# A fused Perceiver block on one Trainium2 core: the third batch's value leaf sum on TensorE, and its attention's last steps moved

## What is computed

```
x = x + xattn(layernorm(x), ctx, ctx)                     # 16 heads of 64, context 4 x 2048 x 128
x = x + retention(layernorm(x))                           # 8 heads of 16: Q K^T * decay, V, group norm, silu gate, W_O
x = x + ffn(layernorm(x))
...
def _fff(x, nw, nb, w1, b1, w2, b2, act):                 # 8 decisions choose one of 256 leaves for each row
    for _ in range(DEPTH):
        node = 2 * node + 1 + (logit > 0)
    h = act(einsum('bsd,bsdl->bsl', x, w1[leaf]) + b1[leaf])        # 16 hidden values for each row
    return einsum('bsl,bsld->bsd', h, w2[leaf]) + b2[leaf]          # the leaf sum: 16 weighed blocks and a bias
...
q, k, v = _fff(xn, ...q), _fff(xn, ...k), _fff(xn, ...v)
att = softmax(q @ k.T / sqrt(D))
y = xn + att @ v
return y + _fff(y, ...f, gelu)
```

## Time and profile before

| what | us |
|---|---|
| median of 3 runs | 679.15 (678.81 to 680.03) |
| the profiled execution, its own time | 679.74 |
| its span in the profile | 677.5 |
| PE busy | 608.1 (90%) |
| DVE busy | 450.5 (66%) |
| ACT busy | 394.6 (58%) |
| POOL busy | 280.4 (41%) |

### The profile page before, as it was taken

How to read it: one execution, slowest core, us unless ns; L and a number is a source line. 1 busy time by engine, 2 the same in 40 slices (tenths; PEclk the granted TensorE clock), 3 DMA queues, 4 the chain that set the end, 5 groups by cost and what they waited for, 6 DMA issues and landing times.

```text
span 677.5 us, 10771 instructions
## 1 busy us (share of the span) xinstructions
PE 608.1 (90%) x4122; PEld 536.2 (79%) x4122; DVE 450.5 (66%) x799; ACT 394.6 (58%) x837; POOL 280.4 (41%) x267
## 2 busy tenths in 40 slices
PE   5899999999999999898999999989999998865664
PEld 3688888999998989777988898777989897744554
DVE  1666656777776776776777777776778776842833
ACT  2765555677664555866556855957557755521541
POOL 3210002021110207996162438876161548944832
PEclk9999999999999999998999999999999999975795
DMA  9710000020100008130030045300300052103812
GB/s 200 218 33 1 1 0 1 1 63 32 32 1 1 1 2 320 31 99 1 1 129 1 1 147 239 118 13 1 126 4 1 5 222 99 66 1 128 352 51 119
DMA packets 21401, 48.52 MB, mean 72 GB/s; under 512 B 1508, under 2 KB 14696, under 8 KB 17256
## 3 DMA queue, kind: packets, MB, share of 16 engines
q0 software_dynamic: 4608, 34.74, 13.6%
q1 hardware_dynamic: 16024, 12.79, 7.1%
q10 hardware_dynamic: 720, 0.33, 0.2%
HBM read 47.59 MB, written 0.26 MB: 71 GB/s over the span
## 4 chain that ended last, share of the span: by engine, by line
PE 65%; POOL 16%; DVE 7%; ACT 6%; issue 3%; DMA 2%; ACTq 0%; POOLq 0%; DVEq 0%
PE ps_s L428 24%; PE ps_av L428 20%; PE ps_ring L648 13%; POOL leaf L1417 6%; PE ps_m L428 4%; PE ps_ring L428 3%; POOL leaf L1421 3%; ACT prob L977 2%; POOL leaf L1458 2%; DVE chunk_max L1268 2%; POOL ct_lo L1386 1%; DVE pt_lo L1062 1%; ACT pt_hi L905 1%; DMA leaf<-up_f_dram,idx 1%; POOL leaf L1399 1%
## 5 line engine op out<-in xcount | busy, mean ns | idle before, releaser
L905 ACT CAST pt_hi<-ps_ring 128x512 fp32r<-128x512 f32 x256 | 144.5, 590 | 149.5 <-PE ps_ring L648 147.3
L1062 DVE TENSOR_TENSOR pt_lo<-ps_ring,pt_hi 128x512 fp32r<-128x512 f32 x256 | 170.4, 686 | 63.2 <-ACT pt_hi L905 63.1
L648 PE MATMUL ps_ring<-ident,prob 128*128 128x128 f32 x1024 | 145.2, 274 | 14.5 <-DVE x_sb L1300 4.9
L977 ACT ACTIVATE prob<-ps_s,neg_max 128x1024 f32<-128x1024 f32 x128 | 141.7, 1113 | 27.4 <-DVE neg_max L1351 27.2
L1268 DVE TENSOR_REDUCE chunk_max<-ps_s 128x1 f32<-128x1024 f32 x128 | 150.7, 1216 | 4.5 <-PE ps_s L428 4.4
L428 PE MATMUL ps_av<-pt_hi,c_hi 128*128 128x256 f32 x512 | 151.3, 295 | 0.0
L648 PEld LDWEIGHTS ps_ring<-ident,prob 128*128 128x128 f32 x1024 | 117.2, 141 | 41.3 <-issue 23.6
L428 PE MATMUL ps_av<-pt_lo,c_hi 128*128 128x256 f32 x512 | 144.7, 283 | 0.0
L428 PE MATMUL ps_av<-pt_hi,c_lo 128*128 128x256 f32 x512 | 144.6, 282 | 0.0
L428 PE MATMUL ps_s<-ct_hi,q_hi 128*128 128x512 f32 x256 | 113.4, 443 | 5.1 <-ACT prob L977 3.5
L428 PE MATMUL ps_s<-ct_hi,q_lo 128*128 128x512 f32 x256 | 102.1, 399 | 0.0
(11 more groups left out here) (264 smaller groups left out, 747.5 us busy)
## 6 DMA issues: line engine op xcount, KB each, us to landing
stage<-ctx_t_dram SPq DMA_DIRECT2D x16, 256.0 KB, 3.4
stage<-ctx_rows_dram SPq DMA_DIRECT2D x16, 256.0 KB, 3.0
leaf<-w_v_dram SPq DMA_DIRECT2D x1, 512.0 KB, 8.1
leaf<-w_o_dram SPq DMA_DIRECT2D x1, 512.0 KB, 10.8
dec<-decay_dram SPq DMA_DIRECT2D x1, 512.0 KB
nw<-node_w_dram SPq DMA_DIRECT2D x1, 510.0 KB
wsm<-w_small_dram SPq DMA_DIRECT2D x1, 448.0 KB
leaf<-wq_t_dram SPq DMA_DIRECT2D x1, 384.0 KB, 11.3
```

What stands on the lines that cost most here:

```text
L648: last = nc.tensor.transpose(o[:, i * P:(i + 1) * P], prob[:, n % 2, k:k + P], ident[:])
L905: nc.scalar.copy(pt_hi[:, pp, row:row + KPC, P * (n % 2):P * (n % 2 + 1)], ps_ring[:, i % 2, :].rearrange("p (k q) -> p k q", k=KPC)).then ...
L977: nc.scalar.activation(prob[:, n % 2, 1024 * e:1024 * (e + 1)], ps_s[:, 1024 * e:1024 * (e + 1)], ACT.Exp, bias=neg_max[:, n:n + 1], accum ...
L1062: return nc.vector.tensor_tensor(o, a, b_, op)
```

## The change

The third batch's value leaf sum goes from POOL to PE. `value_sum(True)` (step `v_half`) adds the bias and the 8 blocks that POOL has weighed, `value_sum(False)` (step `v_rest`) the 8 blocks that ACT has weighed, in a free part of the PSUM bank `ps_av`; ACT then copies the sum to `tree[:, 2, :]` (`v_sum_copy`). POOL's `fold2` and `out2` of this batch get the number 1000, which no slot has: they are not issued. The numbers of steps of the third batch behind the scores of its attention are raised: `attv`, `y`, `res`, `y_t`, `logits_f`, `turns_f`, `path_f`, `pick_f`.

```diff
 BEFORE_LAST_AT = {
-    ("PE", "qk_t"): 72, ("PE", "att"): 73, ("PE", "attp_t"): 76, ("PE", "attv"): 76, ("PE", "y_t"): 78,
-    ("PE", "logits_f"): 79, ("PE", "path_f"): 80,
-    ("ACT", "qk_t"): 73, ("ACT", "att"): 76, ("ACT", "attp_t"): 77, ("ACT", "y_t"): 78, ("ACT", "gelu"): 91,
+    ("PE", "qk_t"): 72, ("PE", "att"): 73.5, ("PE", "v_half"): 73, ("PE", "v_rest"): 76, ("PE", "attp_t"): 76, ("PE", "attv"): 77.5, ("PE", "y_t"): 80,
+    ("PE", "logits_f"): 81, ("PE", "path_f"): 82,
+    ("ACT", "qk_t"): 73, ("ACT", "att"): 76, ("ACT", "attp_t"): 77, ("ACT", "v_sum_copy"): 78, ("ACT", "y_t"): 81, ("ACT", "gelu"): 91,
...
-    ("DVE", "attmax"): 75, ("DVE", "y"): 77, ("DVE", "turns_f"): 80, ("DVE", "pick_f"): 82, ("DVE", "hid3"): 90,
-    ("Pool", "res"): 78, ("Pool", "gather3"): 83, ...
+    ("DVE", "attmax"): 75, ("DVE", "y"): 80, ("DVE", "turns_f"): 82, ("DVE", "pick_f"): 83, ("DVE", "hid3"): 90,
+    ("Pool", "res"): 82, ("Pool", "gather3"): 83, ...
...
-    ("Pool", "fold2"): 74,
-    ("Pool", "out2"): 74,
+    ("Pool", "fold2"): 1000,
+    ("Pool", "out2"): 1000,
 }
...
+            def value_sum(by_pool):
+
+                rows, o = down_rows_at(B - 2, 2), ps_av[:, 2 * P:3 * P]
+                if by_pool:
+                    pe.wait_ge(S["av_taken"], PAIRS)
+                    pe.wait_ge(S["got_down2"], 16 * (B - 1))
+                    mm(o, ident[:], rows[:, W1:DOWN_ROW], True, False)
+                    pe.wait_ge(S["v_weighed"], 1)
+                    for l in range(LW // 2, LW):
+                        mm(o, ident[:], rows[:, D * l:D * (l + 1)], False, False)
+                else:
+                    pe.wait_ge(S["weighed"], 4 * (B - 2) + 3)
+                    for l in range(LW // 2):
+                        last = mm(o, ident[:], rows[:, D * l:D * (l + 1)], False, l == LW // 2 - 1)
+                    last.then_inc(S["v_summed"], 1)
...
+                elif k in ("v_half", "v_rest"):
+                    value_sum(k == "v_half")
...
+                elif k == "v_sum_copy":
+                    act.wait_ge(S["v_summed"], 1)
+                    nc.scalar.copy(tree[:, 2, :], ps_av[:, 2 * P:3 * P]).then_inc(S["v_out_ready"], 1)
...
                 if b == B - 1:
                     weighed.then_inc(S["down_ready"], 1)
+                elif (b, t) == (B - 2, 2):
+                    weighed.then_inc(S["v_weighed"], 1)
...
                 pool.wait_ge(S["weighed"], 4 * b + t + 1)
-                if (b, t) == (B - 2, 2):
-                    pool.wait_ge(S["xn1_ready"], B)
```

More of the change, by code:

```diff
@@ L62 @@
 BEFORE_LAST_AT = {
-    ("PE", "qk_t"): 72, ("PE", "att"): 73, ("PE", "attp_t"): 76, ("PE", "attv"): 76, ("PE", "y_t"): 78,
-    ("PE", "logits_f"): 79, ("PE", "path_f"): 80,
-    ("ACT", "qk_t"): 73, ("ACT", "att"): 76, ("ACT", "attp_t"): 77, ("ACT", "y_t"): 78, ("ACT", "gelu"): 91,
+    ("PE", "qk_t"): 72, ("PE", "att"): 73.5, ("PE", "v_half"): 73, ("PE", "v_rest"): 76, ("PE", "attp_t"): 76, ("PE", "attv"): 77.5, ("PE", "y_t"): 80,
+    ("PE", "logits_f"): 81, ("PE", "path_f"): 82,
+    ("ACT", "qk_t"): 73, ("ACT", "att"): 76, ("ACT", "attp_t"): 77, ("ACT", "v_sum_copy"): 78, ("ACT", "y_t"): 81, ("ACT", "gelu"): 91,
     ("ACT", "down3"): 92,
-    ("DVE", "attmax"): 75, ("DVE", "y"): 77, ("DVE", "turns_f"): 80, ("DVE", "pick_f"): 82, ("DVE", "hid3"): 90,
-    ("Pool", "res"): 78, ("Pool", "gather3"): 83, ("Pool", "up3"): 1000, ("Pool", "weigh3"): 1000, ("Pool", "fold3"): 1000,
+    ("DVE", "attmax"): 75, ("DVE", "y"): 80, ("DVE", "turns_f"): 82, ("DVE", "pick_f"): 83, ("DVE", "hid3"): 90,
+    ("Pool", "res"): 82, ("Pool", "gather3"): 83, ("Pool", "up3"): 1000, ("Pool", "weigh3"): 1000, ("Pool", "fold3"): 1000,
     ("Pool", "out3"): 1000,
@@ L323, in program @@
             q0_done q0_ready ct_split c_split s_done negmax_ready exp_done ring_filled ring_free
-            ring_taken block_ready own_ready third_blocks third_sum sum_done v_copied roped root_ready gain_ready scaled ysq_ready wv_centred qmask_last hi_done av_done av_taken dve_link pool_link wv_turned wvt_ready wvo_done wvo_ready xn1_ready xn1t_done
+            ring_taken block_ready own_ready third_blocks third_sum sum_done v_copied v_weighed v_summed roped root_ready gain_ready scaled ysq_ready wv_centred qmask_last hi_done av_done av_taken dve_link pool_link wv_turned wvt_ready wvo_done wvo_ready xn1_ready xn1t_done
             xn1t_ready gatedt_ready xft_ready qkt_ready apt_ready yt_ready qk_done qk_copied
```

## The result

| | before | changed |
|---|---|---|
| median of 10 runs each | 678.37 us (675.24 to 680.82) | 674.02 us (672.45 to 676.69) |
| ratio of the two, 95% interval | | 0.9941 (0.9918 to 0.9963) |
| profiled execution, its own time | 679.74 | 673.01 |
| span | 677.5 | 671.0 |
| PE, DVE, ACT, POOL busy | 608.1, 450.5, 394.6, 280.4 | 607.8, 449.1, 394.8, 275.0 |

The changed kernel is faster by 4.35 us, 0.6%; by the interval 2.5 to 5.6 us. The forecast was 673.6, with 5.55 us of gain.

A forecast was written before the change was run, and what follows sets the result against it. Bound: a cross-engine chain behind the heads, PE idling for POOL's value sum and then running at half clock. 5.9 - 0.15 - 0.2 = 5.55 off 679.74 gives 674.2; median 0.6 lower, so 673.6, range 672.5 to 676.5.

The forecast's parts named there:

- Item 1: v_half on PE, 18 instructions, 2.1 us, fits PE's free time in 593.0 to 597.3: cost 0.
- Item 2: v_rest on PE, 16 instructions ahead of score0, costs 1.87 us; score0 then starts at 601.50.
- Item 3: Without POOL's additions, DVE's qk_x takes 0.42 instead of 1.34 and qmask 0.69 instead of 1.10; mask at 601.15.
- The rival with POOL first: POOL's half of the mask starts first and holds DVE: 0.7 to 1.0 lost, 674.5; DVE-held-up chance 0.16.
- Item 4: Scores and yv at full clock, yv 1.95, ending 606.33; square at 606.36, 5.9 us earlier.
- My sign for this term: In the new profile, PE's granted clock stays at 1.00 until yv ends at about 606.3.
- the clock falls early: Rival: yv alone at half clock loses 1.65 (675.3, chance 0.13); scores too, 1.8 more (677.1, chance 0.09).
- My split of the 5.9: Square's earlier start: 2.7 from scores starting earlier, 3.3 from clock; 1.1 gained by reordering and 1.1 lost again.
- Items 5 and 6: Gate behind decay1 costs 0.1 to 0.2, taken as 0.15; res ahead of index and gathers costs 0.2.
- first term: The 5.9 us by which square was to start earlier, before subtracting 0.15 and 0.2.
- The index: Path index ready about 609.4, POOL wants it at 610.5; rival that it comes too late, chance 0.04.
- Item 7: From root2 to the end, same instructions and order: worth 0, give or take half a microsecond.

The follow-up runs named there:

- the order alone: Kernel before with the raised step numbers of the change, value sum left on POOL: 678.01 us, ratio 0.9990 against the kernel before.
- before filled once: Kernel before plus 14 unread identity matmuls behind the transposes of batch 2's probabilities: 677.93 us, ratio 0.9988 against the kernel before.
- five variants: Changed kernel with old step order (674.28 us), dummy POOL additions (673.51), gate fillers (672.86), also last-sum fillers and old res place (670.24), then 12 matmuls behind wo (671.05).
- before filled twice: Kernel before plus 14 unread matmuls behind the transposes and 9 ahead of att of batch 2: 675.91 us, ratio 0.9965 against the kernel before.
- The run with POOL kept busy: Changed kernel, POOL again making three additions (1024, 512, 256 wide) on rows nobody reads: 673.51 us, ratio 0.9934 against the kernel before.
- with 12 matmuls behind `wo`: Changed kernel with unread matmuls in gate section and around last sum, res at old place, 12 behind wo: 671.05 us, ratio 0.9906 against the kernel before.
- the kernel with 8: Changed kernel with unread matmuls in gate section (8 behind wo) and ahead of last sum, res at old place: 670.24 us, ratio 0.9898 against the kernel before.

## Why the prediction was right

The forecast held: 673.6 against 674.02, inside the range. The closeness of 0.4 is luck: the gain is 1.2 smaller than forecast (4.35 for 5.55), and the median of the kernel before that I started from was 0.8 too high (679.15 of three runs, 678.37 of ten). What made the gain is what the sum said, the wait for POOL and the clock. Step by step, each time counted from the last transposes (599.52 before, 598.93 now).

**Item 1, `v_half` at no cost.** Right in time, 2.17 for the 18 instructions, and the transposes come 6.03 after `av_sb`, 6.10 before. But "cost 0" leaves out what work in this gap does for the clock. Five profiles have nothing in it (three of before, the order alone, before filled once): PE idles for 1.60 there, and in three of the five the clock fell before the transposes were done, at 598.9, 600.4 and 596.5. Nine profiles have 18 instructions in it (three of the changed kernel, one of each of its five variants, one of before filled twice): in none did the clock fall before `yv`, 12.2 after `av_sb` at the earliest. I had counted the gap only as room.

**Item 2, `v_rest`.** `score0` 1.98 after the transposes by the sum, 1.90 measured.

**Item 3, DVE without POOL's additions.** 0.42 and 0.69, as taken. The run with POOL kept busy shows the cause. The Trainium skill (SBUF — State Buffer, section "SBUF: two separate sides") has a VectorE instruction with two SBUF inputs and a GpSimd one that reads SBUF exclude each other for a whole instruction, with the first to start keeping the shared ports. The rows agree: DVE's mask started 0.04 ahead of POOL's and kept its 0.69, and POOL's stretched by 0.50, a little less than the 0.65 that DVE still ran. In before filled once, DVE's `qk_x` started between two of POOL's additions and took 0.43. The rival with POOL first did not come in any of three profiles of the changed kernel.

**Item 4, scores and `yv`.** `yv` starts after 4.78 (4.86 in the sum), but takes 2.35 instead of 1.95, and `square` comes after 7.17, not 6.84. This term was mis-sized by 0.4: it had the clock up until `yv` ends, and it fell at 605.1. My sign for this term, the clock at 1.00 until `yv` ends, did not come. It is the milder half of the rival "the clock falls early" with 0.4 of the 1.65 that I gave it. It is not the same in each execution: `yv` took 2.35, 1.96 and 2.14 in the three profiles. With two unread matmuls ahead of it the idle time is 0.34 instead of 0.78, and `yv` took 1.96 in all three kernels that have them; but it took 1.96 without them too, in the changed kernel's second profile and with POOL busy, so that the filling undoes the loss is not shown. Counted from `av_sb`, `square` is 5.65 earlier (18.85 and 13.20), against the forecast 5.9. My split of the 5.9 into 2.7 for the start and 3.3 for the clock agrees in kind with the kernel that was filled twice, 3.7 by its profile. The rest there is 1.8, less than 2.7, since `attv` and `decay1` take back part of the earlier start, as the sum said.

**Items 5 and 6.** The gate cost nothing instead of 0.15: POOL's third product ended at 606.45 and `norm` on POOL, released by DVE's `var`, started at 606.99, 0.89 behind the start of `square` (0.88 before). `res` and the gathers cost 0.14 instead of 0.2 (`norm` on POOL to `root2`: 5.84 against 5.70). 5.65 - 0.01 - 0.14 = 5.50, for a forecast of 5.55; the 0.25 that is missing in the first term and the 0.2 that the other two cost less nearly cancel.

**The index.** It was there at 609.53, 0.5 ahead of POOL. I had 609.4 and 610.5, so the margin was half of what I thought.

**Item 7, nothing behind `root2`.** 0.48 shorter in the first pair, within the half microsecond; over the three profiles of each it is 0.35 longer on average (58.22 before, 58.57 changed), and what moves it is the same each time. The last sum got shorter: its last 32 instructions took 6.68 and 6.78 in the first two profiles of before and 5.41, 5.80 and 5.48 in the changed kernel, where the clock rises sooner in it. And DVE's product on the rows of v starts later, 24.81, 24.81 and 24.35 after `root2` before and 25.75, 25.93 and 26.02 in the changed kernel, since the transfer of these rows takes longer (9.9 to 10.4 from its issue before, 11.5 to 11.7 changed). Why it does is open; before filled twice has 11.9. In the chain of the changed kernel DVE waits for it:

```profile
626.86 11.70 DMA leaf<-up_v_dram,idx
638.56 0.02 issue
638.58 1.36 DVE leaf L1083
```

**The size by the medians** is 4.35, not 5.55. The sum was made against one profiled execution of before whose own time, 679.74, lies 1.4 above the median of ten; with three times shown I took the offset as 0.6. The three profiles of each kernel say where most of the missing 1.2 is. On average the stretch from `av_sb` to `root2` is 5.24 shorter (24.97 and 19.73), which is 0.3 less than forecast, since before lost less to the clock in its third profile. What follows `root2` is 0.35 longer and what leads up to `av_sb` 0.1 longer, which leaves 4.8. The remaining 0.45 is within what three profiles can tell, and the interval of the medians is 2.5 to 5.6.

## What to carry to other kernels

In this kernel idle time of TensorE cost twice: the wait, and the half clock for what comes behind it. The clock alone was about half of the gain. A filling is free only while it ends before the wait does: the one that found the clock down took 4.10 instead of 3.29 and held up `attv` by 1.6. Before moving work to shorten a wait, ask what would keep PE busy through it, and at which earlier gap the clock is lost. Measure such a change by the length between two fixed instructions in several profiles; totals of single executions spread by more than half a per cent.

## What the runs showed that I had not expected

- The clock can fall with PE at work. In two profiles of the changed kernel it fell within `yv`, at 605.1 and 607.4, with an idle time of 0.78 ahead of `yv`; in the other at 606.0, in the 0.37 for which PE idles behind `y_t`. In one of the kernel before, at 598.9, during projections that ran without a pause, after a stretch in which PE had worked 2.05 of 4.50 us. The same kernel in another execution kept it to 602.8.
- The same filling did not always hold it: with 12 matmuls behind `wo`, the clock fell at 606.8, ahead of them, where the kernel with 8 had held it to 616.2. In front of the last sum it held to 661.4 in the one and fell at 657.1 in the other, with the same filling there.
- It comes back during steady work: in the kernel that was filled once it rose between 603.0 and 603.5 (0.70 in that half microsecond, 1.00 in the next), in the middle of the 28 instructions, with PE at work since 598.68; in the third profile of before it rose at 609.1, inside `yv`.
